# Attention and routed feed-forward on one core: the lead of the row maxima grows unit by unit instead of in one jump

## The reference

```python
q, k, v = heads(layernorm(x) @ w_qkv)              # 2 batches, 16 heads of 8 columns, 1024 tokens
scores = q @ k.T / sqrt(8)                         # causal mask: -inf above the diagonal
scores += head_scales * (q . dirs) * (k . dirs)    # a bias of rank one per head
out = softmax(scores) @ v                          # per head
x = x + layernorm(out @ w_out)
x = x + layernorm(ffn(layernorm(x)))               # experts
```

## Time and profile before

| | us |
|---|---|
| median of three runs (475.3, 480.36, 480.52) | 480.36 |
| the profiled execution | 473.17 |
| its span, first to last instruction | 471.4 |

### The profile page before, as it was taken

The page is one execution under the profiler, slowest core; times in us unless marked ns, Lnnn a source line. Parts: engine busy times, 40 slices in busy tenths (PEclk is TensorE's granted clock), DMA queues, the critical chain, the costliest instruction groups (busy, mean ns, idle before and its releaser), DMA issues. The chain is left out here.

```text
span 471.4 us, 10711 instructions
## 1 busy us (share of the span) xinstructions
PE 412.6 (88%) x3820; PEld 239.9 (51%) x3820; DVE 320.5 (68%) x1110; ACT 259.7 (55%) x465; POOL 182.3 (39%) x333
## 2 busy tenths in 40 slices
PE   1868999799999999999998698989999999999860
PEld 0532233123323323323342365546999999899860
DVE  2999779889999999998938737697233333233242
ACT  1531577178788788788878267452234443333223
POOL 5034344112312312312554225442676767653302
PEclk9995589699999999999999979899999999999995
DMA  4182215120112102000000091000877877877142
GB/s 117 41 268 95 69 37 171 65 71 2 32 39 71 51 20 71 3 1 3 4 3 2 0 265 49 2 0 12 260 232 232 241 231 231 241 196 234 45 157 89
DMA packets 38711, 46.57 MB, mean 99 GB/s; under 512 B 5315, under 2 KB 26180, under 8 KB 38660
## 3 DMA queue, kind: packets, MB, share of 16 engines
q1 hardware_dynamic: 34580, 39.34, 27.4%
q0 software_dynamic: 2432, 4.99, 3.9%
q10 hardware_dynamic: 1648, 1.57, 1.0%
HBM read 34.80 MB, written 10.88 MB: 97 GB/s over the span
## 5 line engine op out<-in xcount | busy, mean ns | idle before, releaser
L750 ACT ACTIVATE probs<-banks 128x1024 f32<-128x1024 f32 (+1 forms) x192 | 153.2, 812 | 46.2 <-PE banks L586 29.3
L572 PE MATMUL banks<-k_st,q_st 48*128 48x512 bf16 (+3 forms) x384 | 110.9, 355 | 10.1 <-DVE mx_part L870 2.3
L870 DVE CUSTOM_DVE_ANT_0 masked<-banks,mask_max 128x512 bf16<-128x512 f32 (+3 forms) x256 | 110.5, 487 | 12.7 <-PE banks L572 11.4
L586 PE MATMUL banks<-q_st,k_st 51*128 51x512 bf16 (+3 forms) x384 | 101.3, 345 | 4.8 <-DMA q_st<-mx_rows 2.6
L614 PE MATMUL banks<-probs,v_ones 128*9 128x128 f32 (+3 forms) x1536 | 96.7, 337 | 0.3 <-POOL probs L477 0.2
L873 DVE TENSOR_REDUCE mx_part<-banks 128x1 f32<-128x512 f32 x128 | 77.8, 680 | 3.8 <-PE banks L572 3.5
L572 PEld LDWEIGHTS banks<-k_st,q_st 48*128 48x128 bf16 x384 | 31.7, 95 | 93.8 <-DVE mx_part L873 32.4
L477 POOL TENSOR_SCALAR_AFFINE_SELECT probs<-probs 128x256 f32<-128x256 f32 x128 | 52.0, 412 | 63.5 <-ACT probs L750 32.1
L1654 DVE TENSOR_TENSOR hidden<-banks,gate 128x512 f32<-128x512 f32 x38 | 26.3, 691 | 67.8 <-PE banks L1292 67.8
L1167 POOL DMA_INDIRECT results<-result,target x38 | 37.4, 984 | 31.9 <-DVE result L1662 31.9
L614 PEld LDWEIGHTS banks<-probs,v_ones 128*9 128x9 f32 x1536 | 25.6, 90 | 39.8 <-issue 27.9
(11 more groups left out here) (203 smaller groups left out, 476.9 us busy)
## 6 DMA issues: line engine op xcount, KB each, us to landing
w_g<-in_w_gate SPq DMA_DIRECT2D x38, 256.0 KB
w_u<-in_w_up SPq DMA_DIRECT2D x38, 256.0 KB
q_st<-q_rows SPq DMA_DIRECT2D x32, 96.0 KB, 2.3
k_st<-k_rows SPq DMA_DIRECT2D x32, 96.0 KB, 2.4
w_d<-in_w_down SPq DMA_DIRECT2D x8, 256.0 KB, 4.7
back<-results SPq DMA_DIRECT2D x4, 512.0 KB, 7.7
k_rows<-parts SPq DMA_DIRECT2D x6, 256.0 KB, 2.6
q_rows<-parts SPq DMA_DIRECT2D x3, 384.0 KB, 2.6
```

The lines of the kernel that those rows point to most:

```text
L572: nc.tensor.matmul(max_bank[e % RING][:, 0:width], q_st[g][rows, c, p, (i % CH) * P:(i % CH + 1) * P], k_st[g][rows, kc, p, 0:width], star ...
L586: last = nc.tensor.matmul(dst[a][:, 0:BANK - first], k_st[g][rows, j // CH, p, (j % CH) * P:(j % CH + 1) * P], q_st[g][rows, c, p, first:B ...
L750: last = nc.scalar.activation(probs[s % PROBS][:, 2 * p:2 * p + 2, first:BANK], slot_pair[at % 2].rearrange("p (a t) -> p a t", a=2)[:, :, ...
L870: nc.vector.tensor_tensor_reduce(masked[e % RING][:, 0:width], src, mask_max[:, BANK - width:], 1.0, NEG, ALU.add, ALU.max, accum_out=dst) ...
```

## The change

The lead still goes from 8 to 12, but one unit at a time: a maxima-only step stands ahead of s = 2, 5, 8 and 11 (m = 10, 14, 18 and 22), so that the lead is 12 from s = 11. The four maxima-only steps in a row ahead of s = 16 (m = 24 to 27) are gone, and those units ride beside s = 12 to 15. Item 4's maxima (m = 16 to 23) are now all done by step s = 11, so its entry in `TURNED_ALONE` goes, and they are turned beside s = 13 in the score's slot, as for the other items. All matmuls and reductions are the same and as many, and DVE takes the maxima in the same order.

```diff
     steps = [(None, m) for m in range(AHEAD_FIRST)]
+    ahead = AHEAD_FIRST
     for s in range(len(SCORES)):
-        if s == NG * CH:
-            steps += [(None, s + m) for m in range(AHEAD_FIRST, AHEAD_LATER)]
-        m = s + (AHEAD_FIRST if s < NG * CH else AHEAD_LATER)
+        if ahead < AHEAD_LATER and s % (CH - 1) == CH - 2:
+            steps.append((None, s + ahead))
+            ahead += 1
+        m = s + ahead
         steps.append((s, m if m < len(MAXIMA) else None))
     return steps
...
-TURNED_ALONE = {0: CH + CH // 2, NG: NG * CH + AHEAD_FIRST + CH // 2}
+TURNED_ALONE = {0: CH + CH // 2}
```

## The result

| | before | after |
|---|---|---|
| median of 12 runs, us | 479.32 (471.38 to 483.77) | 480.31 (477.4 to 481.42) |
| profiled execution, us | 473.17 | 480.24 |
| its span, us | 471.4 | 478.5 |
| mean granted clock over the span | 0.939 | 0.907 |

The ratio of after to before is 1.0131, with a 95% interval of 1.009 to 1.0171: the changed kernel is slower. That ratio leaves out runs more than 1.5% above the best of their kernel, which of the kernel before are half of the runs, at 480 to 484 us; the medians of all runs differ by 0.2% only. What parts the runs of the kernel before is shown by the first experiment.

A forecast was written before the change was run, and what follows sets the result against it. DVE's reductions were taken to set the pace, its idle time lying in two holes between 47 and 98 us. 3.5 + 2.7 - 0.6 = 5.6 us off the median 480.36 gave 474.8 us, range 464.5 to 481.

The forecast's parts named there:

- The second term: Half-clock units before 66 us: more maxima ride there, unit 13's last reduction comes sooner; gain 2.7 us, bounds 0 to 5.5.
- The sign that was to go with it: DVE's waits before 66 us would be at about 2.8 us if the forecast was right.
- The first term: Wait at unit 16: item 4's maxima turned three units early, all three DVE waits go; gain 3.5 us, bounds 2.2 to 3.5.
- The third term: Maxima 26 and 27 between narrow scores of units 14 and 15 add DVE waits; cost 0.6 us, bounds 0 to 2.3.
- the two extra steps behind 66 us: Maxima-only steps at m = 18 and 22: DVE has no idle time there, so PE and ACT waiting costs nothing.
- the clock would be at 1.00 from the low sixties on: Sign of being right: PE's clock 1.00 from the low sixties to 220 us, no slice near 82 to 94 below it.
- The price per us of low clock: DVE lost 5.5 us in the 14.9 us from 47.6 to 62.5 at half clock, 0.37 us for each.
- the clock that falls again: Rival: low clock through units 8 to 15 and item 4's first unit, 10.6 us lost against 5.6 won, 485.4 us; 7%.
- The rival of rows behind the stores: Item 4's rows queue behind undrained stores on SP's queue, so the 3.5 us are lost: 478.3 us; chance 3%.

The follow-up runs named there:

- the first experiment: The kernel before, run once more with no edit; six runs, the profiled one took 480.54 us.
- lead 12: Changed kernel with the lead at 12 from the first score unit on, maxima 8 to 11 taken alone at the start: 469.73 us, ratio to before 0.9907.
- the late growth: Changed kernel with the lead growing ahead of units 7, 8, 9 and 10 instead of 2, 5, 8 and 11: 478.97 us, ratio to before 1.0109.
- the single step: Changed kernel with a lead of 11 from the start and one maxima-only step, ahead of unit 11: 470.83 us, ratio to before 0.9979.
- the doubled scores: Changed kernel with each score matmul of units 0 to 15 made twice into the same place: 478.62 us, ratio to before 1.0115.
- the two-step kernel: Changed kernel with a lead of 10 from the start and maxima-only steps ahead of units 2 and 5 only: 476.33 us, ratio to before 0.9963.

## Why the prediction was wrong

The forecast was 474.8 us, a gain of 5.6; the kernel got slower.

*The base and the terms were of two different courses of the clock.* The terms were read from the execution of 473.17 us and applied to a median of 480.36, of which two of three runs lie at 480.4 to 480.5. Later runs of the same kernel have such times at clocks of 0.907 and 0.908, where the profiled execution has 0.939.

*The second term, more maxima at half clock, was right as far as it went.* Unit 13's last reduction was to begin at about 59.8 instead of 62.50; it began at 60.16:

```profile
60.16 0.56 DVE L872 CUSTOM_DVE_ANT_0 masked<-banks,mask_max 128x384 bf16<-128x384 f32 x1 [0.99 <-PE banks L574]
```

DVE was ahead by 2.3 us at that point. The sign that was to go with it, waits of about 2.8 us before 66, did not come: they are 5.9 us, since at 0.50 DVE waits again right behind (1.15 us at 61.88 and 1.25 at 65.02).

*The first term was too large.* Of the 3.5 us of waits behind the jump I put all down to the wait for the rows and the jump's low clock, and had all of it go. The rows alone were worth 1.5 us, as the experiment with item 4's rows sent earlier shows, and as the 0.47 us in place of 1.98 after the change shows too. The rest is half clock, and it stayed: DVE's waits from 100 to 120 are 2.9 us at the plain tiles.

*The third term, 0.6 for the narrow maxima, was too small at this clock.* DVE's six waits from 90 to 100 are 4.5 us, 2.0 of them at maxima 26 and 27, which the term was for.

*The step that failed* is the sentence that the two extra steps behind 66 us "only make PE and ACT wait for DVE, which costs nothing", together with the forecast that the clock would be at 1.00 from the low sixties on. Both took one good execution's clock for a property of the kernel. What the runs showed in its place: the step at unit 11 took the clock from 1.00 to 0.50 in the changed kernel, and it did so as the only step, where 10 us were then low (79.3 to 89.5) and DVE's waits were 9.1 us against 5.1 with lead 12 and no step. In every trace in which the clock was up when such steps came behind unit 0, nine with the changed kernel, it fell in them or within 2 us behind: both of the kernel before, the late growth (at its second step), both kernels with matmuls ahead of unit 0 (in the changed one twice), the rows sent earlier, the single step, and the doubled scores (twice). Without such steps, in the traced execution of the lead-12 kernel, it stayed up. They are not all that can bring a fall: it came without one in the two-step kernel at 87.6 and, in the old order with matmuls ahead of unit 0, at 56.

The price per us of low clock, 0.37, was about right (0.32 to 0.39 us of DVE's waits by the traces, 0.4 us of the whole by the runs). In the changed kernel 20 us were low behind unit 11 and 17 more ahead of 79, against 10 at the old jump: 27 us more, 10.8 by the estimate of 0.4, less the 1.5 for the rows 9.3, and DVE stood idle 9.0 us more. Only the 20 us are laid to a step here. Whether the extra steps at units 2 and 5 held the clock back to 79 is not shown: in traces that have them it came back at 73 (scores doubled), 79, 81 and 85 (matmuls ahead of unit 0), and in traces without any step or added matmul up to there at 62 to 67 four times and at 87 twice.

*The rival that came true* was the first, the clock that falls again, at 485.4 with a chance of 7%; its places (units 8 to 15 and the start of item 4) and its decision point, 15 us of low clock behind 62, held. Its price of 5 us for the change is near what was measured, 7.1 us between the profiled executions and 1.3% in the ratio; its 485.4 was 5 us above the measured 480.3 because the base already had such runs in it. For it I had quoted the Trainium skill, "TensorE: Matmul & The Clock Gate", section "A second HAM failure mode: psum-queue depth-cycling", of a PE that pauses between groups of matmuls as it cycles through banks. The trace agrees with it: 0.21 us of waiting ahead of each maxima matmul from the step's third on, and the clock down 2 us behind the step. The evidence that I had held against it, 66 to 82 us at 1.00 with DVE at its limit, was of units with scores between the maxima.

*The rival of rows behind the stores* is out: PE has no wait for rows at unit 16, in the changed kernel or in the lead-12 kernel, where the clock was up.

*What stays open.* Why the clock takes so long to come back in the one-chunk items, from 62 in one execution to 87 in another of the same program, while PE is busy by the record nearly all the time; what in PE's work brings it back; why the same matmuls at the same distances let it fall in the two-step kernel and not with lead 12; and why 32 added matmuls of 128 rows kept it away in both profiled executions while 64 doubled scores did not. The runs show that PE's busy time is not the answer, and no more. That the spread of the runs is one of chance in the moment when the clock returns was only argued, from runs of one program that differ in it.

The kernel with a lead of 12 from the start has the lowest median of all: 469.73 us, 0.9907 of before (0.9859 to 0.9955).

## What to carry to other kernels

Before a sum is built on a stage where PE's granted clock changes, look at the runs' mean clocks: if they differ and the times follow them, a change acts on the clock's course first, and the waits of one trace are those of one course. The base to which a difference is applied must be of the same course. A row of matmuls that all wait for another engine is not free because that engine sets the pace; it can cost the clock of the work behind it, so work done to get ahead belongs where the clock is low anyway, here ahead of the first scores. The mean clock of a run is not enough, either: what counted here was the low time beside the scores. And a term can be right in its place, as the second was, while the state that the sum assumes does not hold.

## What the runs showed of the hardware

- Ahead of 86.0 us in the changed kernel, where the clock fell from 1.00 to 0.50, PE had maxima matmuls at DVE's pace, one each 0.6 us with 0.21 us of waiting, and was busy 1.43 and 1.57 of 2 us by the record. In the single-step kernel the same row brought the fall at 79.3.
- With other matmuls between the maxima, PE busy 6.00 and 5.84 of 6 us, the clock was 1.00 from 36 to 48 us; without them, busy 5.17 and 4.43, it was 0.50.
- The same matmuls at the same distances came with a fall in one kernel (two steps, 87.6) and without one in another (lead 12, 81 to 82).
- At 0.50 PE can be busy 5.6 to 6.0 of each 6 us for 70 us on end and not be granted the higher clock (48 to past 120 us with the added 128-row matmuls). The first two-chunk item, with 512-wide scores and maxima, had it back within about 4 us in the kernel before (92.4 to 96.2) and 6.4 in the changed kernel (100.0 to 106.4).
- One program had its clock back at 62 us in one execution (473.17 us) and at 87 in another (480.54).
